# Top-p attention in a graph kernel: a step-two search with two narrow first trials and one fine trial less

## What is computed

```python
q = X @ W1.T @ W2.T;  k = X @ W3.T
probs = softmax(q @ k.T)
idx = argsort(-probs);  sp = probs sorted;  cs = cumsum(sp)
mask[idx] = cs - sp < 0.9
A = probs * mask / sum(probs * mask)

R = (adj + I) / row sums
for n in range(2):
    A  = top_p_attention(Xa)
    Xf = R @ Xf
    Xa = A @ Xa
    Z  = Z + Xf @ U1[n].T + Xa @ U2[n].T
out = layernorm(x + layernorm(x + Z) * g + b)
```

## Time and profile before

| | us |
|---|---|
| median of three runs | 1677.75 (1675.21 to 1677.92) |
| the profiled execution | 1674.65 |
| its span in the profile | 1672.9 |
| VectorE busy | 1420.2 (85%) |
| TensorE busy, matmuls | 1235.2 (74%) |
| ScalarE busy | 873.1 (52%) |

### The profile page before, as it was taken

The page is one execution under the profiler, slowest core; times in us unless marked ns, Lnnn a source line. Parts: engine busy times, 40 slices in busy tenths (PEclk is TensorE's granted clock), DMA queues, the critical chain, the costliest instruction groups (busy, mean ns, idle before and its releaser), DMA issues.

```text
span 1672.9 us, 29438 instructions
## 1 busy us (share of the span) xinstructions
PE 1235.2 (74%) x9162; PEld 1052.3 (63%) x9162; DVE 1420.2 (85%) x7461; ACT 873.1 (52%) x1633; POOL 179.1 (11%) x357
## 2 busy tenths in 40 slices
PE   6978888888889918896979883929590917457860
PEld 3756676667777817786878773828580816456860
DVE  3688888888856789997989898989898989988987
ACT  2677767766656634655555552525452534425430
POOL 0110000000001411222121210000000100000000
PEclk8999999999999968998989896959795968778885
DMA  5100000000022310413224140311130110303101
GB/s 175 42 1 1 2 1 2 2 1 2 2 83 83 138 68 8 158 42 124 83 83 122 43 165 1 124 42 61 64 108 16 53 72 13 111 1 124 41 2 41
DMA packets 16589, 96.41 MB, mean 58 GB/s; under 512 B 1251, under 2 KB 8930, under 8 KB 9730
## 3 DMA queue, kind: packets, MB, share of 16 engines
q1 hardware_dynamic: 16384, 94.14, 16.0%
HBM read 92.43 MB, written 1.70 MB: 56 GB/s over the span
## 4 chain that ended last, share of the span: by engine, by line
DVE 58%; PE 27%; issue 7%; ACT 6%; SPq 2%; DVEq 1%; DMA 0%; ACTq 0%
DVE junkC L746 14%; PE bank L523 14%; DVE cand L703 13%; PE bank L502 6%; DVE E L1076 6%; DVE E L1074 5%; PE bank L487 5%; ACT E L593 3%; DVE slots L801 2%; DVE sub L902 2%; DVE junkS L746 1%; DVE st L755 1%; DVE st L754 1%; DVE st L756 1%; PE bank L538 1%
## 5 line engine op out<-in xcount | busy, mean ns | idle before, releaser
L620 ACT ACTIVATE blkT<-bank 128x512 f32<-128x512 f32 (+1 forms) x728 | 413.1, 568 | 526.6 <-PE bank L502 523.0
L703 DVE MAX8 cand<-E 128x8 f32<-128x32 f32 (+1 forms) x3172 | 413.2, 211 | 42.8 <-ACT E L583 42.2
L502 PE MATMUL bank<-ident,E 128*128 128x128 f32 x1144 | 193.9, 297 | 322.8 <-DVE E L1076 322.8
L523 PEld LDWEIGHTS bank<-X,blkT 128*128 128x128 f32 x2704 | 335.7, 195 | 131.9 <-issue 65.6
L523 PE MATMUL bank<-X,blkT 128*128 128x128 f32 (+1 forms) x2704 | 379.7, 284 | 47.7 <-ACT blkT L620 46.8
L502 PEld LDWEIGHTS bank<-ident,E 128*128 128x128 f32 x1144 | 151.7, 155 | 328.2 <-DVE E L1076 326.4
L746 DVE SCALAR_TENSOR_TENSOR junkC<-cand,st 128x208 f32<-128x208 f32 (+1 forms) x416 | 303.4, 768 | 3.7
L502 PE MATMUL bank<-ident,S 128*128 128x128 f32 x1560 | 240.1, 273 | 9.5 <-DVE S L1076 5.4
L487 PE MATMUL bank<-kT,Q 64*128 64x512 f32 (+1 forms) x728 | 196.2, 616 | 0.0
L502 PEld LDWEIGHTS bank<-ident,S 128*128 128x128 f32 x1560 | 185.0, 141 | 13.8 <-DVE S L1076 6.0
L523 PE MATMUL bank<-YA,blkT 128*128 128x128 f32 x1352 | 189.3, 284 | 0.0
(11 more groups left out here) (202 smaller groups left out, 1136.7 us busy)
## 6 DMA issues: line engine op xcount, KB each, us to landing
S<-in_adj_dram SPq DMA_DIRECT2D x50, 1663.5 KB, 6.9
S<-in_adj_dram SPq DMA_DIRECT2D x2, 1455.6 KB, 8.9
X<-in_x_dram SPq DMA_DIRECT2D x6, 256.0 KB, 4.5
out_dram<-H SPq DMA_DIRECT2D x2, 768.0 KB
S<-in_adj_dram SPq DMA_DIRECT2D x2, 194.9 KB, 10.1
u_in<-in_L_gnn_U_dram SPq DMA_DIRECT2D x4, 64.0 KB, 9.6
w_in<-in_L_gnn_W_dram SPq DMA_DIRECT2D x2, 32.0 KB, 2.0
X<-in_x_dram SPq DMA_DIRECT2D x1, 64.0 KB
```

Source lines behind the costliest of these rows:

```text
L502: m = pe.transpose(BLK[early][slot][:, b * P:(b + 1) * P], src[:, j * P:(j + 1) * P], ident[:, :])
L523: m = pe.matmul(bank[int(u.acc)][:, 0:width], blkT[:, slot, b * P:(b + 1) * P], rhs[:, j, 0:width], start=(j == 0), stop=(j == NT - 1))
L620: act.activation(blkT[:, slot, 0:w], BLK[early][slot][:, 0:w], ACT.Copy).then_inc(blk_done, 1)
L703: v.max(cand[:, par, xx, 8 * r:8 * r + 8], E[where_e[self.s, self.p]][:, xx, r * w:min((r + 1) * w, N)]).then_inc(s_max, 1)
```

## The change

In step two the first two coarse trials run over the five largest values of each run only (520 values instead of 832), read as groups of five with a step of eight. For that ScalarE makes the exponentials of the candidates in two instructions per tile, one over the ranks 0 to 4 (summed into `csum`) and one over the ranks 5 to 7 (summed into `csum_low`), and VectorE adds `csum_low` to the budget after the second trial. The other five coarse trials stay as they are. The fine trials are two instead of three, so that the interval from which the eight values are taken is twice as wide. `AIM` goes from 20 to 24. Step one does the same work as before.

```diff
-    FINE = [0, 3]
+    FINE = [0, 2]
+
+    FIRST, RANKS = 2, 5
...
-    AIM = 20.0
+    AIM = 24.0
...
+        csum_low = sb("csum_low", [P, 2, 2])
...
             def exp_candidates(gp, s, xx):
                 par = gp % 2
-                act.activation(cand[:, par, xx, 0:NC[s]], cand[:, par, xx, 0:NC[s]], ACT.Exp,
-                               bias=negm[:, par, xx:xx + 1], scale=1.0, accum_out=csum[:, par, xx:xx + 1])
+                pieces = [(0, 8, csum)] if s == 0 else [(0, RANKS, csum), (RANKS, 8, csum_low)]
+                for lo, hi, total in pieces:
+                    c = cand[:, par, xx, 0:NC[s]].rearrange("p (n k) -> p n k", k=8)[:, :, lo:hi]
+                    act.activation(c, c, ACT.Exp, bias=negm[:, par, xx:xx + 1], scale=1.0,
+                                   accum_out=total[:, par, xx:xx + 1])
...
+                def leading(xx):
+                    return c(xx).rearrange("p (n k) -> p n k", k=8)[:, :, 0:RANKS]
+
+                def leading_scratch(xx):
+                    return junkC[:, xx, 0:n // 8 * RANKS].rearrange("p (n k) -> p n k", k=RANKS)
...
-                trials(link, c, scratch, FACT[0:C], FACT[C] if F else 1.0)
+                if s:
+                    trials(link, leading, leading_scratch, FACT[0:FIRST], FACT[FIRST])
+                    link(v.tensor_tensor(two(BUDGET), two(BUDGET), csum_low[:, par, :], ALU.add))
+                trials(link, c, scratch, FACT[FIRST if s else 0:C], FACT[C] if F else 1.0)
```

## The result

The kernel after takes 1672.66 us in the median of 20 runs (1669.19 to 1674.1), the kernel before 1676.78 us (1673.83 to 1679.4). The ratio is 0.9975 (95% interval 0.9968 to 0.9981): 4.1 us faster. The forecast was a gain of 17.9 us; the time lies in the forecast range, but the gain is less than a quarter of the one forecast.

What follows compares the result with a forecast made beforehand. VectorE's own work was taken to set the pace from pair 0 to pair 12. The sum 12.8 - 2.6 + 8.3 - 0.6 = 17.9 us, off 1677.75, gave 1659.9 us; range for 8 in 10: 1653 to 1706.

Steps and rivals of the forecast that it cites:

- The narrow trials: First two coarse trials of step two: sums over 520 instead of 832 values win 12.8 us over 13 pairs.
- the bounds: Strided sums of the narrow trials: 16.8 us won if no value pays a penalty, 3.2 lost if all 520 pay.
- a penalty on every fifth value: Strided sums of the narrow trials: only the fifth value pays, 4.0 us over the 52 sums, leaving 12.8 us.
- The added step: VectorE's chained instruction adding to the budget after the second trial: 0.20 us each, 2.6 us lost over 13 pairs.
- the fine trial: Dropped fine trial of step two: 0.60 us a pair for pairs 0 to 11, 1.13 in pair 12, together 8.3 us won.
- ScalarE: Candidate exponentials in two instructions per tile: 0.28 us added each, hidden except in pair 0, so 0.6 us lost.
- The cover: ScalarE's slack before VectorE needs its exponentials: about 2 of 5.3 us left, nothing charged; up to 4 us if it breaks.
- the wider last interval: Last interval of step two's search, 0.0205 wide: more than eight values there flag 0.1 row more.
- The rival: One more second look: 22.0 us in its own pair, about 18 in a flagged pair (time about 1678); chance 0.25.
- the second trial misled by a missing sixth value: Second narrow trial of step two: a sixth large value missing from the sum flags about 1.2 rows of 3327.
- A new look: Second looks of step two beyond the six before: none 0.53, one 0.25, two or more 0.22.
- looks by misled second trials: Rival of two or more new looks in step two: 22.0 us each, 1703.9 us for two; chance 0.22.

## Why the prediction was wrong

**The narrow trials** were costed rightly in kind and 4 us too low. The measured sum over 520 values is 770 ns, 328 ns less than over 832; 52 of them give 17.1 us where I had taken 12.8. The value that I chose between the bounds, a penalty on every fifth value, was the wrong one; the end without a penalty holds. Of the two readings of the rule in the Trainium skill (SBUF — State Buffer, the note on cachelines) the mean over the group's hits is the one that VectorE's 770 ns for five of eight bear out; a value in eight by itself still costs 1.78 ns. ScalarE, which reads and writes its groups in place, does not agree: its 836 ns over five of eight lie 0.12 us above the 720 that the line through its packed rows (458 ns for 208 values, 981 for 832) gives for 520 values, while 543 ns over three of eight are on that line (545).

**The added step and the fine trial** behaved as costed, taken together: the row maximum came 53.1 us after the head of the search in pair 5 before and 51.35 us after it now; 1.38 us of that were in the sum, and the free strides add 0.33. **ScalarE** cost 0.7 us in pair 0 for the 0.6 forecast; its two instructions last 0.40 us a tile more than the one did, not 0.28, the rest being the five-of-eight groups. **The cover** held in the kernel after, as charged. So without a new look the sum would have been 17.1 - 2.6 + 8.3 - 0.7 = 22.1 us.

**The step that failed** is the number of second looks, in the sentence on the wider last interval: "this adds 0.1 row". It added a tile, and at about 18 us the look took back nearly all: 22.1 - 18 = 4.1 us. The measured median gain is 4.1 us too; that it agrees to the tenth is luck, as the waits behind the branch and the start of step two move by several us from one trace to the next. The rival named the price and the outcome in a flagged pair (a look of about 18 us), but gave it to the wrong part, the second trial misled by a missing sixth value. With five ranks that flags no new tile.

**Why the wider interval flags more** than the estimate allowed: I had taken the values near the cut as independent and spread over the logarithm, so that only rows with some 280 kept values could crowd the interval. Twelve looks with one fine trial, where that picture gave eight or nine, speak against it on the chip. What crowds the interval I worked out on a host from the reference's inputs, in float64, with the search written out in numpy. It gives the chip's numbers of flagged tiles, but no run shows the values themselves, so this cause is argued:

```
flagged tiles   3 fine: 6    2 fine: 7    1 fine: 12    (as on the chip)
row 1619 (tile 12, pair 6) keeps 121; its kept values over the smallest kept:
  ... 1.0113 1.0073 1.0031 1.0031 1.0031 1.0031 1.0031 1.0021 1
row 2323 keeps 34:   1.00024 (ten times) 1 1
rows flagged because eight values don't reach the cut
  3 fine: 2, both in tiles that a too full run flags anyway; 2 fine: 3
rows that keep a single node in step one: 839 of 3327
  (the ten equal values of row 2323 are nodes that all keep node 2710;
   four of the five near 1.0031 in row 1619 are nodes that all keep node 1479)
```

By this working many nodes have equal features in step two, because their attention in step one kept the same single node. Their probabilities are equal in every row, and a group of equal values can sit in the last interval however few a row keeps. The row that flags the new tile is 1619: nine kept values lie within 1.2% of its cut, four of them equal. The kernel says as much: it has code that drops ties. I had that code in front of me and reasoned as if there were none.

**The chances.** A new look had 0.47 together, so the case that came was not a rare one in the forecast, only booked under another cause. That the time still lies in the range (1653 to 1706) comes from that other cause: the range was drawn for looks by misled second trials.

## What to carry to other kernels

A search that ends in "flag it and look again" has two prices, the trial and the look; here a fine trial is worth 0.6 us a pair and a look 18 to 22 us, so one tile of 26 (by the host's working one row of 3327) took back four fifths of the gain. Count the flags of the changed search on the real inputs before costing its instructions, and look for equal values in them first. Take the parts of such a change singly: the narrow trials alone are faster than both kernels, 1661.08 us (ratio 0.9898, 0.9883 to 0.9912), and the missing fine trial alone is a loss.

## What the hardware showed that I had not expected

- A branch that jumps over code leaves VectorE standing still: mostly 3.3 to 3.7 us over 236 and 330 instructions, 1.1 to 1.5 over 151, 0.6 where there is no branch. Every wait of 3.3 us or more has an instruction packet starting in it (53 of 53), no wait under 1.8 us has one (0 of 25). Code that is never run cost this kernel 22 to 24 us: 24 between the medians 1661.08 and 1636.97, 22 by the two ratios.
- Run maxima that were issued just before the jump covered little of it: in step two 41.3 us of waits were left of 46.7.
- Reading five of eight float32 values costs VectorE's sums nothing over packed values (770 ns for 520, where the packed slope gives 774), while one of eight costs 1.78 ns a value. ScalarE pays 0.12 us for the same groups of five (836 ns against 720).
